# Where the scan layers' projection runs each batch's transposes on the TensorE queue

## What is computed

```python
xr, gate = jnp.split(x @ W_in.T, 2, axis=-1)
xr = xr + t_emb[:, None, :]
xc = jax.nn.silu(causal_conv4(xr) + b_conv)       # 4 taps along the sequence, per channel
xn = (xc - mean(xc)) / jnp.sqrt(var(xc) + 1e-05) * ln_g + ln_b
Bm, Cm, dt = jnp.split(xn @ W_xproj.T, 3, axis=-1)
...
return y * jax.nn.silu(gate) @ W_out.T
```

## Time and profile before

| | |
|---|---|
| three runs of the kernel | 3997.74, 4001.2 and 4002.31 us, median 4001.2 |
| span of the profiled execution | 3993.2 us, 8.0 less than the median; its own time beyond the span is not recorded |
| granted clock over the span, share of 2.4 GHz | 0.959 |
| busy time | PE 3737.8 (94%), DVE 3026.1 (76%), POOL 1896.0 (47%), ACT 1334.5 (33%) |
| first projection | from the start to about 497 us |
| second projection | from about 2690 to 3199 us |

### The profile page before, as it was taken

One profiled execution on the slowest core, in us unless ns is written; L12 is line 12 of the kernel. 1 busy time (PEld: TensorE's weight loads), 2 busy tenths in 40 slices (PEclk: granted clock), 3 DMA queues, 4 the chain that ended last, 5 costly groups with the idle time before them and its releaser, 6 DMA issues. The chain is left out here.

```text
span 3993.2 us, 63716 instructions
## 1 busy us (share of the span) xinstructions
PE 3737.8 (94%) x22068; PEld 2291.3 (57%) x22068; DVE 3026.1 (76%) x3176; ACT 1334.5 (33%) x2014; POOL 1896.0 (47%) x1446
## 2 busy tenths in 40 slices
PE   8999769999998789999999999988999859999999
PEld 6777523433333567777777777766777613433334
DVE  4776679999997677777777777744666679999997
ACT  3555411111111444344434444323555501111111
POOL 2655635555554124444444444342555735555554
PEclk9999859999999799999999999999999959999999
DMA  3666755565653323222322222223666765565563
GB/s 121 236 240 246 286 200 169 183 194 173 187 187 120 112 90 128 78 80 79 107 88 91 80 80 80 67 78 121 227 238 245 275 223 169 175 193 179 183 194 112
DMA packets 272125, 630.18 MB, mean 158 GB/s; under 512 B 33216, under 2 KB 35904, under 8 KB 271840
## 3 DMA queue, kind: packets, MB, share of 16 engines
q1 hardware_dynamic: 264816, 615.49, 46.3%
q10 hardware_dynamic: 7104, 11.93, 0.8%
HBM read 390.87 MB, written 241.70 MB: 158 GB/s over the span
## 5 line engine op out<-in xcount | busy, mean ns | idle before, releaser
L1164 DVE CUSTOM_DVE_ANT_0 l0r_g<-l0r_g,l0r_pv,l0r_cf 128x1024 f32<-128x1024 f32 x512 | 674.1, 1339 | 70.4 <-PE l0r_pv L964 46.7
L1164 DVE CUSTOM_DVE_ANT_0 l3r_g<-l3r_g,l3r_pv,l3r_cf 128x1024 f32<-128x1024 f32 x512 | 673.9, 1339 | 68.3 <-PE l3r_pv L964 43.6
L102 PE MATMUL l1h_ps_p<-l1h_xh,l1c_wh 128*128 128x512 f32 x768 | 322.6, 420 | 5.7 <-issue 3.5
L104 PE MATMUL l1h_ps_p<-l1h_xl,l1c_wh 128*128 128x512 f32 x768 | 308.2, 401 | 0.0
L103 PE MATMUL l1h_ps_p<-l1h_xh,l1c_wl 128*128 128x512 f32 x768 | 305.4, 398 | 0.0
L2152 POOL TENSOR_TENSOR l1h_st<-l1h_veps 128x1 f32<-128x1 f32 x64 | 35.4, 554 | 565.5 <-DVE l1h_veps L2010 565.5
L964 PE MATMUL l3r_pv<-l3r_x,l3r_wv 32*128 32x512 f32 x1024 | 260.4, 507 | 25.0 <-POOL l3r_wv L884 17.4
L964 PEld LDWEIGHTS l0r_pv<-l0r_x,l0r_wv 32*128 32x128 f32 x1024 | 97.2, 187 | 324.7 <-issue 205.0
L964 PEld LDWEIGHTS l3r_pv<-l3r_x,l3r_wv 32*128 32x128 f32 x1024 | 96.5, 186 | 324.7 <-issue 191.8
L964 PE MATMUL l0r_pv<-l0r_x,l0r_wv 32*128 32x512 f32 x1024 | 261.7, 510 | 22.5 <-POOL l0r_wv L884 16.4
L976 PE MATMUL l0r_py<-l0r_g,l0r_cd 128*32 128x512 f32 x2048 | 281.7, 624 | 0.0
(11 more groups left out here) (386 smaller groups left out, 9046.9 us busy)
## 6 DMA issues: line engine op xcount, KB each, us to landing
l0r_x<-xhl_s SPq DMA_DIRECT2D x128, 512.0 KB, 11.4
l3r_x<-xhl_s SPq DMA_DIRECT2D x128, 512.0 KB, 11.6
xhl_s<-l0a_xo SPq DMA_DIRECT2D x116, 512.0 KB, 4.6
xhl_s<-l3a_xo SPq DMA_DIRECT2D x116, 512.0 KB, 4.6
gate_s<-l0a_gate SPq DMA_DIRECT2D x64, 256.0 KB, 2.5
l0r_dx<-dx_s SPq DMA_DIRECT2D x32, 512.0 KB, 13.2
l0r_gate<-gate_s SPq DMA_DIRECT2D x32, 512.0 KB, 13.9
l0r_crow<-feed_s SPq DMA_DIRECT2D x64, 256.0 KB
```

The costliest lines, as they stand in the source:

```text
L102: pe.matmul(out, wh, xh, start=first, stop=False)
L104: return pe.matmul(out, wh, xl, start=False, stop=last)
L1164: dve._custom_dve(bass.dve_ops.TENSOR_ADD_SAT, out=g[:, t, j, :], in0=g[:, (t - 1) % TS, j, :], in1=pv[j % 2][:, :], s0=cf[:, q, t, 0, j:j ...
```

## The change

In the loop over the middle tiles (T = 1 to 6) and in the first loop of the last tile (T = 7), `turn(n)` moves from the even step of its pair to the odd one, and there it stands directly behind the input product, ahead of the gate product. The batch number `TB * (T - 1) + it // 2` is the same for both steps of a pair, so the batches keep their order. Nothing is added or removed, and the queues of DVE, ACT, POOL and SP are as they were.

```diff
             for T in range(1, NT - 1):
                 for it in range(KI):
                     project_x(T, it)
+                    if it % 2 == 1:
+                        turn(TB * (T - 1) + it // 2)
                     if rows and it == KI - 1:
                         turn_x(T + 1, TB - 1)
                     project_gate(T, it)
-                    if it % 2 == 0:
-                        turn(TB * (T - 1) + it // 2)
...
             T = NT - 1
             for it in range(KI):
                 project_x(T, it)
-                if it % 2 == 0:
+                if it % 2 == 1:
                     turn(TB * (T - 1) + it // 2)
```

## The result

| | before | after |
|---|---|---|
| median of four runs each, us | 4001.76 (3997.74 to 4005.69) | 3974.22 (3972.19 to 3977.95) |
| span of the profiled execution, us | 3993.2 | 3970.3 |
| that execution's own time, us | not recorded | 3972.19 |
| granted clock over the span | 0.959 | 0.959 |

The ratio is 0.9934, with a 95% interval of 0.992 to 0.9949: 27.5 us less by the medians, 22.9 us less between the two profiled executions. Forecast were 3978.3 us and 22.9 us.

What follows compares the result with a forecast made beforehand. TensorE's queue was taken to pace middle tiles, DVE the last tile. First layer 6.2 + 1.2 + 5.5 = 12.9 us, second 5.7 + 4.3 = 10.0; 4001.2 - 22.9 gives 3978.3 us, range 3971 to 3990.

Steps and rivals of the forecast that it cites:

- First wait of a middle tile: PE's wait ahead of a middle tile's first transposes goes, five tiles a layer: 6.2 us in the first, 5.7 second.
- Wait for the input split: First layer, PE's 0.33 us wait for DVE's split shrinks by 0.12 to 0.33, six times; 1.2 us taken.
- Last tile: DVE's waits for input products go in each layer's last tile: 5.5 us gained in the first, 4.3 in the second.
- POOL's wait as the cushion: First layer, behind the last tile's centring: DVE's 2.86 us idle for POOL's factor leaves room for a 2.4 us delay.
- DVE's 5.87: First layer's last tile: DVE's queue is 5.87 us earlier at the loop's last centring, the upper bound of the gain.
- The rival of a clock that stays low: Low clock through the last tile's gate products in each layer: some 15 us slower, 4016; chance 0.04.
- take over the middle tiles: First layer: POOL's operation catches another DVE split, costing 1.43 us a tile; 13.1 us gained, 3988; chance 0.10.
- the last tile gives nothing: Stores' drain sets the projection's end, so both last tiles are worth nothing: 3.3 us remain, 3998, no change; chance 0.06.
- more than forecast: All of 0.33 six times, 5.87 and no clock loss: 24.1 us gained, about 3973; chance 0.06.
- the 8.0 us that were put on the span: Whole kernel: the median of the runs was 8.0 us above the profiled span, and the forecast kept that.

Runs made afterwards that it cites:

- experiment with the early split: On the changed kernel, first layer: DVE's first input split of a tile is issued before the taps of step 5, not after; 3970.02 us, ratio 0.9929.
- experiment with the early gate product: On the changed kernel: the last tile's first gate product no longer waits for the last input product's evacuation; 3976.67 us, ratio 0.9944.

## Why the prediction was right

**First wait of a middle tile: right, undersized.** The waits went, in both layers. But a period shrank by (274.83 - 267.73) / 5 = 1.42 us in the first layer and by 1.35 in the second, where 1.24 and 1.14 of idle time had been counted. The idle time is counted from the modelled end of the matmul ahead, 0.39 us after its start, while the next one could have started 0.23 after it, as the prediction's own start-to-start figure says. That is 0.16 us a wait, of 0.18 and 0.21 that were missing. The windows agree: counted to modelled ends, PE's busy time in the tile fell as well, by 53.39 - 53.21 = 0.18 us for the same work. Over ten tiles: 13.9 us against 11.9.

**Wait for the input split: wrong.** The step that failed is the term of 1.2 us. It allowed 0.12 to 0.33 us a tile and got nothing. PE's way from the evacuation of step 5 to the next tile was forecast at 15.68 us and is 344.71 - 0.33 - 328.68 = 15.70. DVE's chain, forecast at 15.25 to 15.89, is 343.83 + 0.82 - 328.68 = 15.97. POOL's operation starts 5.81 us after that evacuation where it had started 4.94, because gate product 5 is later and POOL hangs on ACT behind it; the held split ends 8.75 after it instead of 7.90. What PE was pushed back by, the split was pushed back by too, so the wait stayed at 0.33. The prediction named this and priced it, with 15.89 us and 0.21 of the 0.33 left; it should have taken this as the likely case, and POOL's delay as 0.87 and not 0.79, for before the change the split had ended behind POOL's operation already. The experiment with the early split shows it. The Trainium skill, "SBUF — State Buffer", section "Who interferes with whom", has a DVE instruction with two SBUF inputs and a POOL instruction that reads SBUF wait for each other: the split agrees, the taps beside POOL's operation (2.33 us for three) do not.

**Last tile: right.** First layer 5.14 us against 5.5, second 4.87 against 4.3 (this one within the 2 us that it varies by). The order of events was as forecast: 1.25 us of wait instead of 4.06, no wait of DVE for an input product, a long idle time, a low clock behind it, and POOL's wait as the cushion. Of the 0.73 us that the first layer stays behind DVE's 5.87, the experiment with the early gate product gives back 0.21; the rest is there without PE's delay too. What follows hangs on ACT's landed stores still, a wait of 5.66 us where there was 6.89, and 7.52 in that experiment:

```profile
465.61 1.06 ACT L490 ACTIVATE l0a_xo<-l0a_xn 128x1024 fp32r<-128x1024 f32 x1 [5.66 <-DMA xhl_s<-l0a_xo]
```

So of 2.07 us of PE's delay 0.21 came through. That the rest is lost to the landing of the stores is what these rows suggest; no run here moves the stores alone.

**The rival of a clock that stays low** is refuted. One gate product was slow (4.82 us from its first matmul's start to its last's, where the next has 2.57). It was back within that product. The kernel before shows the same more plainly than the prediction read it: input product 7, the first behind the 2.88 us of idle time, began low, with 0.78 us for its first matmul at 444.19; the gate product at 450.06, which the prediction took for the next one, is the one after it. The Trainium skill, "TensorE: Matmul & The Clock Gate", section "Part 1: The HAM clock gate (the "warmup" mystery)", says that an idle engine goes back to the slow level; the trace agrees with the fall, 0.57 in the window of the slow product.

**The other rivals.** DVE did not take over the middle tiles: no further split was caught by the change (the last one of a tile took 0.80 us before and 0.82 after), and the wait stayed at 0.33 us. That the last tile gives nothing falls with the experiment that moves it alone. The time itself, 3974.22, is nearest to "more than forecast" (3973), but not by its reasons: neither the 0.33 us nor the whole 5.87 came.

**The sum.** By the stages 7.10 + 5.14 + 6.76 + 4.87 = 23.9 us against 22.9; the rest of the program was 1.0 us longer in that execution, which makes the spans differ by exactly 22.9, partly by luck: the second layer's first tile took 4.3 us more in it and the last recurrence 4.2 less. The median came out 4.1 us below the forecast for another reason: the 8.0 us that were put on the span. The execution after shows 3972.19 - 3970.3 = 1.9 us around it, and every other execution on record 1.8 to 2.2. With that, the profiled execution before took about 3995.1 us, a quick one, and the 8.0 was mostly its distance from its own median; after, that distance plus the 1.9 is 3.9.

## What to carry to other kernels

On an in-order queue, put an instruction that waits behind as much ready work as its consumer's slack allows, and no further: one product ahead paid here, two gave half to all of it back. Before counting a wait as gone, follow what the move delays on other engines; if the thing that ends the wait hangs on the same delayed product, the wait moves with it. And a span's distance from the median of the runs belongs to that execution, not to the kernel.

## What was not expected of the hardware

A wait on TensorE cost 1.35 to 1.42 us where its idle time read 1.14 to 1.24. DVE's split, held by POOL's operation, ended 0.54 to 0.56 us after it, whether it had begun 0.25 or 0.84 us into it, while the taps on the same engine were not held at all, nor were the second layer's splits, which read PSUM. It is not the operation that decides for the taps: the rescaling at L618 is a SCALAR_TENSOR_TENSOR like the taps, and took 3.35 us where it began beside POOL's L718 and 1.28 where POOL ran no long operation. What sets the taps apart stays open.
